# Second normalisation and rounding moved from the MLP stage of a vision-text block into its attention stage, with another rounding

## Reference

```python
h = concat(patches @ W.T + b, txt)                      # 324 x 256 an image
h = h + attn(layernorm(h))                              # 16 heads of 16, causal, softmax
x = layernorm(h)
q4 = lambda x: grid(x / s) * s    # s = max|x| / 6 of each 16 columns; grid: 0 .5 1 1.5 2 3 4 6
gate, up = q4(x) @ q4(w_gate).T, q4(x) @ q4(w_up).T     # 704 columns each
out = h + q4(silu(gate) * up) @ q4(w_down).T
```

## Time and profile before

| | us |
|---|---|
| median of 3 runs | 2220.32 (2212.43 to 2222.04) |
| profiled execution, its own time | 2218.99 |
| its span | 2217.2 |
| TensorE busy | 1984.9 (90%) |
| VectorE busy | 1738.2 (78%) |
| ScalarE busy | 1057.0 (48%) |
| GpSimd busy | 980.8 (44%) |
| mean granted TensorE clock | 0.948 of full |

### The profile page before, as it was taken

One profiled execution on the slowest core, in us unless ns is written; L12 is line 12 of the kernel. 1 busy time (PEld: TensorE's weight loads), 2 busy tenths in 40 slices (PEclk: granted clock), 3 DMA queues, 4 the chain that ended last, 5 costly groups with the idle time before them and its releaser, 6 DMA issues. The chain is left out here.

```text
span 2217.2 us, 40958 instructions
## 1 busy us (share of the span) xinstructions
PE 1984.9 (90%) x16096; PEld 1580.4 (71%) x16096; DVE 1738.2 (78%) x3071; ACT 1057.0 (48%) x2075; POOL 980.8 (44%) x699
## 2 busy tenths in 40 slices
PE   3899999999999999999999848888888888888888
PEld 3687777777787777878777536666666666666666
DVE  5677777777777776676766349999999999999995
ACT  1355555555555554545454324444444444444443
POOL 6223232323232322232322016666666666666664
PEclk8899999999999999999999769999999999999997
DMA  5474747464656565565644021111111111111100
GB/s 117 70 96 82 95 82 95 82 93 84 91 87 91 86 87 90 78 99 77 100 66 67 14 62 34 36 37 36 36 37 37 40 39 36 36 36 36 36 30 29
DMA packets 129909, 142.02 MB, mean 64 GB/s; under 512 B 19894, under 2 KB 124854, under 8 KB 129718
## 3 DMA queue, kind: packets, MB, share of 16 engines
q1 hardware_dynamic: 122806, 138.40, 35.8%
q10 hardware_dynamic: 6912, 1.00, 0.3%
HBM read 51.25 MB, written 23.40 MB: 34 GB/s over the span
## 5 line engine op out<-in xcount | busy, mean ns | idle before, releaser
L532 DVE TENSOR_REDUCE maxima<-maxp 108x2 f32<-108x648 f32 (+2 forms) x448 | 415.6, 928 | 281.5 <-PE maxp L802 279.8
L711 ACT ACTIVATE probs<-expp 108x648 f32<-108x648 f32 (+2 forms) x512 | 364.5, 712 | 417.8 <-PE expp L831 401.3
L1115 POOL TENSOR_TENSOR q_b<-t_b,m_b 128x960 f32<-128x960 f32 (+2 forms) x85 | 192.5, 2265 | 272.0 <-DVE t_b L1177 272.0
L827 PE MATMUL expp<-qst,kst 99*108 99x324 bf16 (+2 forms) x1536 | 264.0, 264 | 25.5 <-ACT probs L711 12.3
L799 PE MATMUL maxp<-kst,qst 96*108 96x108 bf16 (+2 forms) x1536 | 265.6, 265 | 19.9 <-DMA kst<-parts 12.3
L451 POOL TENSOR_TENSOR rest<-qkf,parts 128x648 f32<-128x648 f32 x64 | 90.9, 1421 | 403.5 <-ACTq L684 403.5
L799 PEld LDWEIGHTS maxp<-kst,qst 96*108 96x108 bf16 x1536 | 163.8, 130 | 97.5 <-DVE maxima L532 48.4
L827 PEld LDWEIGHTS expp<-qst,kst 99*108 99x108 bf16 x1536 | 158.8, 130 | 92.2 <-ACT probs L711 33.8
L59 PE MATMUL gu<-wgu_hi,xqT 128*128 128x512 f32 (+1 forms) x486 | 215.8, 444 | 6.7 <-ACT xqT L1285 6.7
L851 PE MATMUL attp<-probs,vblk 108*32 108x324 f32 (+2 forms) x3072 | 219.1, 366 | 0.0
L802 PE MATMUL maxp<-mask_qk,identb 108*108 108x108 bf16 (+2 forms) x896 | 215.8, 247 | 0.0
(11 more groups left out here) (194 smaller groups left out, 5023.9 us busy)
## 6 DMA issues: line engine op xcount, KB each, us to landing
qst<-parts SPq DMA_DIRECT2D x192, 162.0 KB, 5.8
kst<-parts SPq DMA_DIRECT2D x192, 162.0 KB, 7.4
patches<-in_xT SPq DMA_DIRECT2D x32, 588.0 KB, 4.6
h_dram<-h_rows SPq DMA_DIRECT2D x32, 324.0 KB
xt<-h_dram SPq DMA_DIRECT2D x81, 128.0 KB, 2.3
res<-h_dram SPq DMA_DIRECT2D x81, 128.0 KB, 2.0
out_rows<-ot SPq DMA_DIRECT2D x81, 128.0 KB, 2.0
h<-in_txt SPq DMA_DIRECT2D x32, 108.0 KB
```

Of the source, the lines that this page charges most:

```text
L532: dve.tensor_reduce(rowmax[half][:, h:h + nh, c].rearrange("p (a h) -> p a h", a=2), src, AX.X, ALU.max).then_inc(maxp_free, 1)
L711: act.activation(dst, expp[0:CH, 0:banks, 0:per * w], ACT.Exp, scale=SCALE).then_inc(expp_free, 1)
L827: pe.matmul(expp[0:CH, a, x * w:(x + 1) * w], kst[s][0:ROWS + NPART, h, kc * CH:(kc + 1) * CH], qst[s][0:ROWS + NPART, h, kc * CH:T], star ...
```

## The change

It takes the second layer norm and the rounding of its rows out of the MLP stage and does them in the attention stage, a new third sub-step for image n-3, in 108-partition rows; the finished rows go to DRAM as xq, beside h1. The new steps "x2 ..." stand in STEPS between the others. One more iteration is run at the end. The rounding is done another way: y = x / (long scale), sq = Square(ROOT * y) in bf16 on ScalarE, t = (sq + ADDEND) + y, q = (sq + ADDEND) - t, which is the negative of the rounded value, and one GpSimd product with the whole scale. In the MLP stage the rounded rows are loaded, turned in full float32, and split once from PSUM: ScalarE takes the high part with its sign turned, VectorE the low part. The same goes for the hidden values, and the sum with the residual reads the down product from PSUM. There is one gu buffer in place of two, and the pipeline has six steps, unrolled. The weights' rounding is not changed. Shortened:

```diff
-SCALE_HI_BITS = 0xFFFFC000
+ADDEND = 1.375 * 2.0 ** 22
+ROOT = (5 / 32 * 2.0 ** 22) ** 0.5
+LONG = 1.0 + 2.0 ** -22
...
+        self.finishes = on(it - 3)
...
-    for it in range(-1, n_images + 2):
+    for it in range(-1, n_images + 3):
...
-    MAX_A[0], ("xnT", 0), ("xnT", 1), ("attend", 1, 0), ("exp", 2, 0), MAX_A[1], ("exp", 2, 1), ("tok", 1),
-    ("attend", 1, 1), MAX_A[2], ("w", 0), ("qk", 0), ("attend", 1, 2), MAX_A[3], ("exp", 2, 2), ("qk", 1),
-    MAX_A[4], ("exp", 2, 3), ("w", 1), ("qk", 2), MAX_A[5], ("w", 2), ("exp", 3, 0), ("attend", 2, 0),
-    ("tok", 1), ("w", 3), ("tok", 1), MAX_A[6], ("w", 4), ("exp", 3, 1), ("attend", 2, 1), ("attend", 2, 2),
-    ("w", 5), ("exp", 3, 2), ("neg", 0), ("qk", 3), ("tok", 1),
+    MAX_A[0], ("x2 stats",), ("xnT", 0), ("xnT", 1), ("attend", 1, 0), ("exp", 2, 0), MAX_A[1], ("exp", 2, 1),
+    ("x2 norm",), ("tok", 1), ("attend", 1, 1), MAX_A[2], ("w", 0), ("qk", 0), ("attend", 1, 2), MAX_A[3],
+    ("x2 scale",), ("exp", 2, 2), ("qk", 1), MAX_A[4], ("x2 y",), ("exp", 2, 3), ("w", 1), ("qk", 2), MAX_A[5],
+    ("w", 2), ("exp", 3, 0), ("attend", 2, 0), ("x2 t",), ("tok", 1), ("w", 3), ("tok", 1), MAX_A[6], ("x2 q",),
+    ("w", 4), ("exp", 3, 1), ("attend", 2, 1), ("attend", 2, 2), ("w", 5), ("exp", 3, 2), ("neg", 0), ("qk", 3),
+    ("tok", 1),
...
+        x2n = sb("x2_n", [CH, NC * D])
+        x2_t = x2_out = x2n
+        x2_y = x2_q = xn[:].rearrange("p c d -> p (c d)")
+        x2_sq = att[:].rearrange("p c d -> p (c d)").bitcast(BF16)[:, 0:NC * D]
...
+                if k.finishes:
+                    sp.wait_ge(x2_out_done, n - 2)
+                    sp.dma_start(xq_dram[n - 3], x2_out[:].rearrange("p (c d) -> p c d", d=D)).then_inc(x2_stored, 16)
...
+                def x2_products():
+                    pool.wait_ge(x2_q_done, n - 2)
+                    pool.tensor_tensor(blocks(x2_out[:]), blocks(x2_q), spread(x2_scale[:], CH, NB2),
+                                       ALU.mult).then_inc(x2_out_done, 1)
+                if k.finishes:
+                    pool.wait_ge(x2_aggr_done, n - 2)
+                    pool.tensor_tensor(x2_vareps[:], x2_meanvar[:, :, 1], eps[0:CH, :],
+                                       ALU.add).then_inc(x2_vareps_done, 1)
+                    pool.wait_ge(x2_vareps_done, n - 2)
+                    pool.tensor_tensor(x2_rstd[:], x2_vareps[:], minus_half[0:CH, :], ALU.pow).then_inc(x2_rstd_done, 1)
+                if k.qkv:
                     rest_of(0)
+                if k.finishes:
+                    x2_products()
+                if k.qkv:
                     rest_of(1)
...
+                def x2(step):
+                    done = n - 2
+                    what = step[0]
+                    if what == "x2 stats":
...
+                        for c in range(NC):
+                            ins = dve.bn_stats(x2_stats[:, c, :], h1[:, c, :])
+                        ins.then_inc(x2_bn_done, 1)
+                        dve.wait_ge(x2_bn_done, done)
+                        for c in range(NC):
+                            ins = dve.bn_aggr(x2_meanvar[:, c, :], x2_stats[:, c, :])
+                        ins.then_inc(x2_aggr_done, 1)
+                    elif what == "x2 norm":
+                        dve.wait_ge(x2_rstd_done, done)
+                        dve.scalar_tensor_tensor(x2_shift[:], x2_meanvar[:, :, 0], -1.0, x2_rstd[:], ALU.mult,
+                                                 ALU.mult).then_inc(x2_shift_done, 1)
+                    elif what == "x2 scale":
+                        dve.wait_ge(x2n_done, done)
+                        dve.tensor_reduce(x2_amax[:], blocks(x2n[:]), AX.X, ALU.max,
+                                          apply_absolute_value=True).then_inc(x2_amax_done, 1)
+                        dve.wait_ge(x2_amax_done, done)
+                        dve.tensor_scalar(x2_long[:], x2_amax[:], LONG / 6.0, SCALE_MIN * LONG, ALU.mult,
+                                          ALU.max).then_inc(x2_long_done, 1)
+                        wait(dve, x2_out_done, done - 1)
+                        dve.tensor_scalar(x2_scale[:], x2_amax[:], 1.0 / 6.0, SCALE_MIN, ALU.mult,
+                                          ALU.max).then_inc(x2_scale_done, 1)
+                    elif what == "x2 y":
+                        dve.wait_ge(x2_long_done, done)
+                        dve.reciprocal(x2_inv[:], x2_long[:]).then_inc(x2_inv_done, 1)
+                        dve.wait_ge(x2_inv_done, done)
+                        wait(dve, x2_out_done, done - 1)
+                        dve.tensor_tensor(blocks(x2_y), blocks(x2n[:]), spread(x2_inv[:], CH, NB2),
+                                          ALU.mult).then_inc(x2_y_done, 1)
+                    elif what == "x2 t":
+                        dve.wait_ge(x2_sq_done, done)
+                        dve.scalar_tensor_tensor(x2_t[:], x2_sq, ADDEND, x2_y, ALU.add,
+                                                 ALU.add).then_inc(x2_t_done, 1)
+                    else:
+                        dve.wait_ge(x2_t_done, done)
+                        dve.scalar_tensor_tensor(x2_q, x2_sq, ADDEND, x2_t[:], ALU.add,
+                                                 ALU.subtract).then_inc(x2_q_done, 1)
...
+                    wait(dve, x2_out_done, n - 2)
...
+                def x2_normal():
+                    act.wait_ge(x2_shift_done, n - 2)
+                    wait(act, x2_stored, 16 * (n - 3))
+                    for c in range(NC):
+                        ins = act.activation(x2n[:, c * D:(c + 1) * D], h1[:, c, :], ACT.Identity,
+                                             bias=x2_shift[:, c:c + 1], scale=x2_rstd[:, c:c + 1])
+                    ins.then_inc(x2n_done, 1)
+                def x2_squares():
+                    act.wait_ge(x2_y_done, n - 2)
+                    act.activation(x2_sq, x2_y, ACT.Square, scale=ROOT).then_inc(x2_sq_done, 1)
...
+                    elif step[0] == "x2 norm":
+                        x2_normal()
+                    elif step[0] == "x2 y":
+                        x2_squares()
...
+        gu = ps("gu", [P, 3 * BANK])
+        turn_h = ps("turn_h", [P, 2 * BANK])
+        last_bank = ps("turn_x", [P, BANK])
+        turn_x, down = last_bank[:, 0:D], last_bank[:, D:2 * D]
...
+        XT, XS, G, R, DN, OUT = 0, 1, 2, 3, 4, 5
...
+            for t in range(2):
+                sp.dma_start(xq[t][:], xq_dram[t * P:(t + 1) * P]).then_inc(xq_in[t], 16)
+            for s in range(STEPS_B):
+                t = s + 2
+                if t < NT:
+                    sp.wait_ge(x_turned, t - 1)
+                    sp.dma_start(xq[t % 2][:], xq_dram[t * P:(t + 1) * P]).then_inc(xq_in[t % 2], 16)
...
+                    wait(pool, h_turned, t - 1)
+                    pool.wait_ge(q_done, t + 1)
+                    pool.wait_ge(scale_done, t + 1)
+                    pool.tensor_tensor(blocks(hq[t % 2][:, 0:FF]), blocks(q[:]), spread(scale[:], P, NB_H),
+                                       ALU.mult).then_inc(hq_done, 1)
...
+            def take_lo_of_negative(lo, x, hi):
+                return dve.scalar_tensor_tensor(lo, x, -1.0, hi.bitcast(F32), ALU.mult, ALU.subtract)
+            for s in range(STEPS_B):
+                t = tile(s, XS)
+                if t is not None:
+                    dve.wait_ge(xT_hi_done, t + 1)
+                    take_lo_of_negative(xqT_lo[t % 2][:], turn_x.rearrange("p (j n) -> p j n", n=P),
+                                        xqT_hi[t % 2][:]).then_inc(xT_lo_done, 1)
+                t = tile(s, OUT)
+                if t is not None:
+                    dve.wait_ge(down_done, t + 1)
+                    dve.wait_ge(res_in[t % 2], 16 * (t // 2 + 1))
+                    wait(dve, stored[t % 2], 16 * (t // 2))
+                    dve.tensor_tensor(ot[t % 2][:], down, res[t % 2][:], ALU.add).then_inc(out_done, 1)
+                t = tile(s, R)
+                if t is not None:
+                    dve.wait_ge(sq_done, t + 1)
+                    dve.scalar_tensor_tensor(t_sum[:], sq[:], ADDEND, y[:], ALU.add, ALU.add).then_inc(t_done, 1)
+                    wait(dve, hq_done, t)
+                    dve.wait_ge(t_done, t + 1)
+                    dve.scalar_tensor_tensor(q[:], sq[:], ADDEND, t_sum[:], ALU.add,
+                                             ALU.subtract).then_inc(q_done, 1)
+                t = tile(s, DN)
+                if t is not None:
+                    dve.wait_ge(hT_hi_done, t + 1)
+                    take_lo_of_negative(hqT_lo[:], turn_h[:, 0:FP].rearrange("p (i n) -> p i n", n=P),
+                                        hqT_hi[:]).then_inc(hT_lo_done, 1)
+                t = tile(s, G)
+                if t is not None:
+                    dve.wait_ge(gu_ready, t + 1)
+                    dve.wait_ge(silu_done, t + 1)
+                    dve.tensor_tensor(h[:], silu[:], gu[:, FF:2 * FF], ALU.mult).then_inc(h_done, 1)
```

(69 more changed lines are left out.)

405 lines of the change are left out of this document (75 added, 330 removed).

## The result

The changed kernel takes 2247.62 us (median of 4 runs, 2238.03 to 2255.49), the kernel before 2217.27 in the same comparison: ratio 1.013, 95% interval 1.0102 to 1.0159. It is **slower by 1.3%**, 30 us, where the forecast was 2196 us and faster. It lies past the 2231 us from which the prediction speaks of slower. The profiled execution took 2252.78 us.

What follows compares the result with a forecast made beforehand. TensorE was taken to bound the attention stage and VectorE the MLP stage. From the 2217.2 us span, minus 209 (MLP), plus 186 (attention), plus 2 for the ends: 2196 us; range 2110 to 2270, the forecast's own 2165 to 2235.

Steps and rivals of the forecast that it cites:

- the prediction's own signs of being wrong: Attention stage growing by under 120 us or over 220, or an MLP period outside 8.0 to 9.2 us.
- the loop: MLP stage: VectorE and ScalarE hand each other work, 8.1 us a tile, below TensorE's 8.35.
- the down product keeps its 18 matmuls, 3.26: MLP stage: the down product's TensorE time stays 3.26 us a tile, part of TensorE's 8.35.
- Fill and drain: MLP stage: time beyond the 81 tile periods, setup included, taken as 46 us where it was 51.
- Steps 1 to 3: Attention iteration: waits for rstd, then y, then the square delay exp(2,3); TensorE loses 4.4 us, bounds 3.35 to 4.6.
- step 2: Attention iteration: GpSimd's rest starts at 588.5, VectorE's y comes at 588.8 and is held, ending at 590.8.
- Step 4: Attention iteration: GpSimd's product holds w 5 or neg 0's cast, delaying the maxima's DMAs; 1.0 us, bounds 0 to 1.6.
- Step 5: Attention iteration: a lower TensorE clock costs 0.4 us, bounds 0 to 1.9, nearer to this stage's own 1.00.
- the slow rival: Attention stage: TensorE's stall is 4.6 + 1.6 us and the clock falls to 0.95, 1.9 more; 2263 us, chance 0.16.
- The two short iterations: Attention stage: the two short iterations behind the 29 full ones add 7 us.
- the last image's own iteration: End of the attention stage: an added iteration with nothing beside it, 11 us after subtracting the old store's 3.2.
- two rivals: Square needs table loads, 2236 us, chance 0.06; GpSimd's product holds VectorE passes with one PSUM input, 2265 us, 0.09.

Runs made afterwards that it cites:

- e4: The changed kernel with the down product's last chunk as 64 rows again, as before the change, instead of 128 zero-padded rows: 2255.62 us, ratio 1.0184.
- e5: The e2 kernel with the rounding step x2 q and its GpSimd product also moved behind neg 0: 2024.14 us, ratio 0.9137 to the kernel before.
- e2: The changed kernel with only ScalarE's x2 square moved, from ahead of exp(2,3) to behind exp(3,0): 2176.64 us, ratio 0.9813 to the kernel before.

## Why the prediction was wrong

Both of the prediction's own signs of being wrong came: the attention stage grew by more than 220 us, and the MLP period was under 8.0. The measured time lies outside the forecast's own 2165 to 2235 and inside the wide range to 2270, but only because two errors of opposite sign met: the attention stage was 107 us worse than forecast, the MLP stage 50 better.

**MLP stage, -209 forecast, -259 measured.** The mechanism was right: y at 0.89 us, a period set by something shorter than the held VectorE. TensorE was named as the bound at 8.35 us; the loop was, at 7.87 (forecast 8.1). The failed term is "the down product keeps its 18 matmuls, 3.26": with a last chunk of 128 rows it takes 0.71 us for six, so 2.1, and 3.2 only with the short one (e4). So TensorE's true sum, 7.1, was under the loop's. With the loop's own 8.1 in place of 8.35 the stage would have been 20 us nearer. Fill and drain were over too: 671.8 - 81 x 7.87 = 34 us, forecast 46. Both misses were on the good side.

**Steps 1 to 3: right.** Against the earlier trace rows, shifted by 165.19 us to this iteration's patches_lo, TensorE's scores that started at 587.75 should have come at 427.0; they came at 426.66. 4.4 us lost was forecast, 4.1 it was. Y was held in full by rest, as step 2 had chosen.

**Step 4: the hold right, its price not.** The product did hold the cast of w5, 1.49 us for 0.23. I had priced that hold against 0.3 us of slack at ("exp", 3, 3), and 1.0 us was the result. What is late next is another thing: the maxima's DMAs. TensorE's order reaches exp(0,0) soon behind neg 0, and SP's transfers follow 0.9 to 1.7 us behind the issue where they had 2.1, with the scores 5.4 to 6.5 us behind it where they had about 5.1. The kernel before already waited 7.0 us for these DMAs, a wait that I had in the trace and did not use. In the changed kernel TensorE waits (71.6 - 7.0) / 28 = 2.3 us an iteration more at this place than before, where the forecast had 1.0 for the step; e5 against e2 gives 3.2 us idle once the first gap is gone.

**Step 5: the failed step.** "Nearer to this stage's own row", 0.4 us, with an upper bound of 1.9 from the MLP's 0.95. Measured: 3.8 us, twice the bound. The mean of a stage was the wrong row: the MLP's waits of TensorE, 106.6 us in 72 over the 790 us of the earlier trace rows, are 1.5 us each on average and come once a tile. In the attention stage a wait of 2.6 us or more was mostly followed by 3.4 to 10.2 us at half clock, half of which is lost, and an iteration has one or two such stretches. The idle time by itself was foretold: 5.8 us against 5.4. With the measured clock (3.8 in place of 0.4) my sum becomes 9.2 x 29 = 267 in place of 168, and the total 2196 + 99 = 2295; the MLP's 50 us bring it back to 2245. **So the sign turned on the clock**: without its 99 us the kernel would have been faster than before. Only the slow rival had let the clock fall, and by half of what it did. That rival's point of 7.0 us an iteration was passed (9.6); its 2263 is near the result because the faster MLP makes up for the rest.

**The ends.** The two short iterations and the next cost 10.4 us more (46.1, 38.4 and 30.1 against 39.1, 37.0 and 28.1; forecast 7), the last image's own iteration 15.28 - 3.66 = 11.6 (forecast 11, whose own terms add up to 10.3). The trace has one table load in each stage, ahead of its first tiles, and none in any iteration, and the GpSimd product holds no pass that reads PSUM (hqT_lo 0.95 us, h 0.88): two rivals are out. The Trainium skill, SBUF — State Buffer, "SBUF: two separate sides", says that only VectorE instructions with two SBUF inputs, or in a mode that takes both ports, compete with GpSimd. Y (two inputs, 1.95 us) was held, hqT_lo and h were not, which agrees. W_m (one input, all in SBUF, 1.49) was held too; whether it ran in such a mode, no trace here shows.

## What to carry to other kernels

In a stage whose orders are written out by hand and whose bound engine is 98% busy, passes on the other engines cost by where they stand: put none of a chain that crosses engines ahead of work that the bound engine waits for within the next microseconds, and look also at small DMAs with a deadline and at what other queue starts just behind them. Price each new wait of TensorE with the slower clock that follows it, not only its own length. Where two engines hand each other work in a loop, add up the loop first; one independent instruction taken out of it was worth 0.9 us a tile here.
